# A fifth buffer for streamed weight chunks, paid for by halving a staging tile

## The reference

```
x = x + layernorm(attn(layernorm(x)))
x = x + layernorm(ffn(layernorm(x)))

attn: u = x W_in^T; gates from silu(x W_sel_in^T) W_sel_out^T
      h_t = a_t * h_{t-1} + b_t * u_t          (scan over 4096 tokens)
      y = (c * h + d * dg * u) W_out^T
ffn:  h = bit_linear(x, w1)                    (1024 -> 4096)
      h = silu(depthwise_conv1d(h, width 3))   (over tokens)
      y = bit_linear(h, w2)                    (4096 -> 1024)
bit_linear: activations rounded to 127 steps of their row's maximum,
            weights to -1, 0, 1 by their mean size
```

## Time and profile before

| | us |
|---|---|
| median of the runs shown (two: 3180.75 and 3181.93) | 3181.34 |
| profiled execution, its own time | 3185.16 |
| its span on the slowest core (core 7) | 3183.6 |
| spans of the eight cores | 3160.3 to 3183.6 |
| TensorE matmul busy | 1508.3 (47%) |
| DVE busy | 1479.0 (46%) |
| ACT busy | 1334.6 (42%) |
| POOL busy | 531.6 (17%) |

### The profile page before, as it was taken

One profiled execution on the slowest core, in us unless ns is written; L12 is line 12 of the kernel. 1 busy time (PEld: TensorE's weight loads), 2 busy tenths in 40 slices (PEclk: granted clock), 3 DMA queues, 4 the chain that ended last, 5 costly groups with the idle time before them and its releaser, 6 DMA issues.

```text
span 3183.6 us, 35705 instructions; the slowest of 8 cores (3160.3 to 3183.6 us)
## 1 busy us (share of the span) xinstructions
PE 1508.3 (47%) x8464; PEld 892.0 (28%) x8464; DVE 1479.0 (46%) x5002; ACT 1334.6 (42%) x2201; POOL 531.6 (17%) x817
## 2 busy tenths in 40 slices
PE   0000026464646464645464646465655556465563
PEld 0000014151414141424242424232333323242240
DVE  1024425463645454454546363626373736273543
ACT  2444434443434444444434344444343434343332
POOL 0000000202020202020212111121212121212202
PEclk9999977677778777878686868787777777777786
DMA  6777600303030303121222212121212131203123
GB/s 206 228 210 217 195 27 1 106 21 106 27 106 27 104 29 91 42 83 50 71 63 60 73 53 80 53 80 54 80 54 80 40 93 37 83 23 97 46 74 99
DMA packets 112701, 260.35 MB, mean 82 GB/s; under 512 B 12656, under 2 KB 12656, under 8 KB 112496
## 3 DMA queue, kind: packets, MB, share of 16 engines
q1 hardware_dynamic: 93200, 196.19, 21.0%
q10 hardware_dynamic: 13824, 41.95, 4.6%
q0 software_dynamic: 5472, 19.93, 2.2%
HBM read 232.85 MB, written 25.17 MB: 81 GB/s over the span
## 4 chain that ended last, share of the span: by engine, by line
PE 23%; DVE 23%; DMA 15%; ACT 14%; issue 10%; DVEq 8%; POOL 4%; ACTq 2%; POOLq 1%; SPq 0%
PE pE L873 8%; DVEq L58 8%; DMA w2sb<-w2s 7%; DVE h L916 4%; PE pD L1062 3%; POOL h L1046 3%; DVE h L924 3%; PE pE L1062 3%; DMA tad<-w2T 2%; DMA tbc<-w2T 2%; DVE h L908 2%; ACT h L888 2%; PE pC L550 2%; ACT hpre L882 2%; PE pB L542 1%
## 5 line engine op out<-in xcount | busy, mean ns | idle before, releaser
L873 PE MATMUL pE<-xqw,w1t 128*128 128x258 bf16 x4352 | 604.9, 303 | 313.7 <-ACT h L888 309.8
L873 PEld LDWEIGHTS pE<-xqw,w1t 128*128 128x128 bf16 x4352 | 461.6, 108 | 440.9 <-issue 340.1
L1062 PE MATMUL pD<-w2sb,h 128*128 128x512 bf16 x1024 | 344.0, 423 | 430.2 <-POOL h L1046 340.8
L882 ACT ACTIVATE hpre<-pE 128x258 bf16<-128x258 f32 x544 | 198.8, 387 | 459.0 <-DVE h L924 358.9
L1046 POOL TENSOR_SCALAR h<-k2i,consts 128x512 bf16<-128x512 int32 x272 | 265.9, 985 | 615.6 <-ACT k2i L1042 615.6
L1062 PE MATMUL pE<-w2sb,h 128*128 128x512 bf16 x1024 | 342.4, 421 | 36.3 <-POOL h L1046 24.9
L1042 ACT ACTIVATE k2i<-h,consts 128x512 int32<-128x512 bf16 x272 | 192.7, 720 | 353.2 <-DVE h L1031 256.6
L1062 PEld LDWEIGHTS pD<-w2sb,h 128*128 128x128 bf16 x1024 | 88.1, 104 | 643.1 <-issue 612.3
L826 DVE COPY xqw<-xqw 128x8 bf16<-128x8 bf16 x16 | 3.0, 186 | 544.4 <-ACT xqw L819 544.4
L908 DVE TENSOR_SCALAR h<-hpre,cwt,cbt 128x256 bf16<-128x256 bf16 x272 | 108.4, 441 | 267.2 <-ACT hpre L882 267.2
L916 DVE SCALAR_TENSOR_TENSOR h<-hpre,cwt,h 128x256 bf16<-128x256 bf16 x544 | 227.5, 480 | 10.3
(11 more groups left out here) (183 smaller groups left out, 2100.3 us busy)
## 6 DMA issues: line engine op xcount, KB each, us to landing
w2sb<-w2s SPq DMA_DIRECT2D x544, 256.0 KB, 3.4
tad<-w2T ACTq DMA_DIRECT2D x32, 512.0 KB, 4.8
xin<-x SPq DMA_DIRECT2D x16, 1024.0 KB, 7.3
tbc<-w2T ACTq DMA_DIRECT2D x32, 512.0 KB, 4.6
stgF<-w1T POOLq DMA_DIRECT2D x32, 512.0 KB, 4.7
stgF<-w1T SPq DMA_DIRECT2D x32, 512.0 KB, 4.8
out<-stgF SPq DMA_DIRECT2D x32, 512.0 KB, 3.1
w2s<-stgb ACTq DMA_DIRECT2D x16, 256.0 KB, 4.6
```

Of the source, the lines that this page charges most:

```text
L873: lambda e, S, c=c, k=k, off=off, pf=pf: e.matmul(pE[:, off:off + 258], w1t[:, 4096 * k + 128 * c:4096 * k + 128 * (c + 1)], xqv[:, pf, k, :],
L882: q.op("a", lambda e, S, c=c, off=off: e.activation(hpre[:, 258 * (c % 4):258 * (c % 4 + 1)], pE[:, off:off + 258], AF.Identity), sem="ac")
L1062: coff=coff: e.matmul(bank[:, 512 * jj:512 * (jj + 1)], h4[:, 256 * c + 128 * s:256 * c + 128 * (s + 1)], w2sb[:, coff:coff + 512], start= ...
```

## The change

`w2sb` gets a fifth slot (5120 columns), with a semaphore of its own (`sw4`). Five chunks are loaded at the start of a window, and chunk c + 5 is issued after chunk c's matmuls. To make room, `stgb` shrinks from 2048 to 1024 columns: both half-tiles now use the same columns, and POOL waits for the first half-tile's transposes (`PE_T2[i][0]`) before it converts the second. SBUF use in total stays the same. Cut to its core:

```diff
-        stgb = sb("stgb", [128, 2048], BF16)
+        stgb = sb("stgb", [128, 1024], BF16)
-        w2sb = sb("w2sb", [128, 4096], BF16)
+        w2sb = sb("w2sb", [128, 5120], BF16)
@@ attn_gen, last part
             for s in range(NSUB):
+                if s == 1:
+                    q.wait("g", "pe", PE_T2[i][0])
                 for h in range(2):
...
-                    bsl = stgb[:, 1024 * s + 512 * h:1024 * s + 512 * (h + 1)]
+                    bsl = stgb[:, 512 * h:512 * (h + 1)]
...
-                        stgb[:, 1024 * s + 128 * cc:1024 * s + 128 * (cc + 1)],
+                        stgb[:, 128 * cc:128 * (cc + 1)],
@@ win_gen, issue_w2t
-                if f == 0 and c < 4:
+                if f == 0 and c < 5:
                     q.wait("sy", "swi", sw_w2)
-                if c >= 4:
-                    q.wait("sy", "pe", PE_w2c[f][c - 4])
+                if c >= 5:
+                    q.wait("sy", "pe", PE_w2c[f][c - 5])
                 elif f > 0:
-                    q.wait("sy", "pe", PE_w2c[f - 1][28 + c])
-                swn = "sw%d" % (c % 4)
+                    q.wait("sy", "pe", PE_w2c[f - 1][27 + c])
+                swn = "sw%d" % (c % 5)
                 SW_w2t[f][c] = (swn, q.op("sy", lambda e, S, c=c: e.dma_start(
-                    out=w2sb[:, 1024 * (c % 4):1024 * (c % 4 + 1)],
+                    out=w2sb[:, 1024 * (c % 5):1024 * (c % 5 + 1)],
                     in_=w2s[:, 1024 * c:1024 * (c + 1)]), sem=swn, k=16))
-            issue_w2t(0)
-            issue_w2t(1)
-            issue_w2t(2)
-            issue_w2t(3)
+            for _c0 in range(5):
+                issue_w2t(_c0)
...
-                        coff = 1024 * (c % 4) + 512 * jj
+                        coff = 1024 * (c % 5) + 512 * jj
...
-                issue_w2t(c + 4)
+                issue_w2t(c + 5)
```

More of the change, by code:

```diff
@@ L38, in __init__ @@
                                    "swi", "gd", "gp", "pe", "dv", "ac",
-                                   "ad", "vd", "sw2", "sw3")}
+                                   "ad", "vd", "sw2", "sw3", "sw4")}
     def do(self, qn, f):
@@ L136, in build_program @@
         for s in ("sm", "sx0", "sx1", "so", "sw0", "sw1", "swi", "gd", "gp",
-                  "pe", "dv", "ac", "ad", "vd", "sw2", "sw3"):
+                  "pe", "dv", "ac", "ad", "vd", "sw2", "sw3", "sw4"):
             sems[s] = st_.enter_context(nc.semaphore(s))
```

## The result

The changed kernel takes 3136.04 us (median, 3134.11 to 3141.65) beside 3181.5 us of the kernel before in the same comparison. The ratio is 0.9855 with a 95% interval of 0.9842 to 0.9867, so 42 to 50 us less, 45.5 by the medians. The forecast was 3153 us with a range of 3130 to 3176.

The account below looks back on a forecast made before the run. No engine bounds it: a string of dependent stages, where w2sb load waits count in chunks 12 to 31. Savings 21.0 + 2.4 + 3.0 + 1.9 = 28.3 us off 3185.2 give 3156.9, less 3.8 for the median: 3153 us, range 3130 to 3176.

Parts of the forecast that it names:

- The place: Second product: of 96.3 us load waits, 71.1 count, mostly in chunks 12 to 31; 25.2 in chunks 0 to 11 don't.
- the cores agree: Support for the place: core 0 waited 67.5 us and ended at 3160.3, core 7 85.1 us and 3183.6.
- The side costs: Halved stgb and POOL's added wait for the first transposes, which ACT's order already makes it meet: cost 0.
- SP's extra issue: SP's queue: one load per window moves into the burst ahead of the window, total loads unchanged: cost 0.
- The mechanism: Second product's load loop: five periods equal landing + 0.86 + 0.47 us; period from 1.158 to 1.04 us.
- 2b: Load loop: landing falls to 2.5 us, all stalls go, 66.6 us saved, 3115 us; chance 0.04.
- 3: Load loop: bandwidth limits, period stays 1.158 us, only the stored chunk wins, 6 us saved, 3175 us; chance 0.17.
- 4: Load loop: landings grow faster than the queue, kernel slower; break-even landing 4.5 us; chance 0.04, 0.02 beyond 2%.
- rival 1: Load loop, the forecast: more in flight, each landing later, about half the stall left, 3145 to 3162 us; chance 0.62.
- rival 2a: Load loop: landing stays 3.3 us, period 0.926, 50.5 us saved, 3131 us; chance 0.13.
- so 3.31 becomes 1.99: Chunks 12 to 31, mean listed waits per window: stall per chunk 0.30 to 0.18 us; stored chunk makes it 1.8.
- the fourteen: Chunks 12 to 31 of windows 1 to 14: 1.5 us saved in each, 21.0 us together.

## Why the prediction was right, and where it was off

**The place was right.** The first part's gain is waited for again and the second part's goes through: both were tried alone, and the stages show it. The mean end of window 16's second product moved from 3156.4 to 3111.2 us, 45.2, of which the stages of the table hold 43.3.

One support of it was weak: that "the cores agree" was read from two of them. Core 4 listed the most, 89.7 us on the pD line, and ended at 3168.5, so the listed waits do not order the cores.

**The side costs were right.** `stgb` and POOL's wait were priced at nothing, with ACT's order as the cover; the halved tile alone measured 0.999, and the releaser and the 6.93 us gap are unchanged (the sixteen gaps are those of tiles 0 to 15, not 1 to 15). SP's extra issue was priced at nothing too. It was not tried alone; that the end moved by as much as the stages became shorter, 45.2 and 43.3 us, leaves no room for a cost.

**The mechanism was right.** Forecast were a landing up to about 3.9 us, a share near 0.9 and a period of 1.04 us between bounds of 0.926 and 1.158; the window shown has 4.0 us, 0.88 and 0.998 us. The mean over windows 1 to 14 and all cores, 1.031 us, is nearer to the forecast than this window. There the loop can be followed load by load, for the loads into the slots of chunk 16 and later: from a chunk's first matmul to the issue of the load into its slot 1.10 us before and 1.11 after, landing 3.37 and 3.76, from landing to the chunk's first matmul 0.21 and 0.31, in sum 4.68 us for four periods and 5.18 for five. The landing rose a little less than forecast (3.87 at a period of 1.04). Rivals 2b, 3 and 4 fall with these rows. The result lies between rival 1 and rival 2a, but not because the landing held still. What the prediction cites from the Trainium skill (section "Anatomy of one DMA") is a fit for DMAs issued by GpSimd, which it does not say; SP issues these loads, and no term of the sum hangs on it.

**The term that was mis-sized is the stall.** The step "so 3.31 becomes 1.99", and then 1.8, took the mean of the listed waits for the whole stall of a second part. The kernel without loads shows 24.08 - 19.58 = 4.50 us there. The share left was well forecast: 1.8 of 3.31 is 0.54, measured 21.76 - 19.58 = 2.18 of 4.50, 0.48. From chunk 19 on the stall went from 3.35 to 1.85 us, 0.55 of it where the forecast had 0.6. In chunks 12 to 18 it went from 1.16 to 0.33 us: there the one more chunk in store won 0.83 us, where the forecast had one stall of 0.18. The window shown hid this, because its store lasted to chunk 19 both before and after; mostly it ran out at chunk 17 or 18 before and at 19 to 22 after. So a second part saved 2.32 us, not 1.5, and the fourteen 32.5, not 21.0. The same undercount runs through the rest: window 15 saved 3.7 (2.4 forecast), window 16 4.4 (3.0), window 0 2.6 (1.9). Sum 43.2 instead of 28.3. The working had the right figure beside the wrong one: thirteen chunks at 0.30 us of stall are 3.9 us for window 6, whose listed waits were 3.0 us; the period was read from start to start and the stall from the list.

**Left open.** Whether the landing grows with the loads of the other cores or with the core's own was not separated: all cores always ran the same depth. The Trainium skill's page "HBM Reference" (section "Specifications") gives a core some 358 GB/s; the fastest stretch shown here reached 318 at an engine share of 0.95, so no run shows that limit. Seven slots differ from six also in the scan's tile, which was not tried alone.

## What to carry to other kernels

Count a stall from start to start of the waiting engine's instructions and against its unstalled pace; listed idle time of a pipelined engine leaves out part of every wait and all of the short ones, here a third. Do not take one window for the mean either. A ring of n buffers that is the limit has the period (landing + use + signal)/n, and the landing grows with n, so read the share of the DMA engines and the landing together: here, with the share below 0.9, each further slot paid, less each time. First find which part of the stage ends last, and look for the room in tiles whose other half is only used after a wait that is there anyway. When the number of slots does not divide the number of chunks, look at the wait at the start of a window too: the changed kernel waits for chunk 27 + c of the window before, but slots 0 and 1 were last read by chunks 30 and 31. What covers this is the order in SP's list, where the output stores of that window stand ahead.

## What the runs showed of the hardware

With 256 KB loads, 2 KB to a partition, and eight cores at work, the 16 DMA engines of a core were 0.65 busy over window 16 with three slots, 0.75 with four, 0.81 with five, 0.85 with six and 0.88 with seven (0.95 in the best stretch shown). I had not expected that it takes so many: four loads of 256 KB look like plenty beside a landing of 3.4 us, and left a quarter of the engines' time unused. The other surprise is the clock in window 16: over the same part of the stage the granted clock was 0.54 with three slots, 0.82 with four, 0.91 with five and 0.92 with six and seven (means over the cores), so longer waits went with a lower clock there. What that adds to the stalls is inside the stage lengths above and was not separated.
